# The transposes of a routed slot's rows, moved behind the transposes of h

## The reference

```
x = x + 0.5 * ffn(layernorm(x))
x = x + attn(layernorm(x))      # w_in, causal conv of 4 taps, linear recurrence of 16 states, silu, w_out
x = x + 0.5 * ffn(layernorm(x))

def ffn(x):                                  # 4096 tokens of 256, F = 512, E = 8 experts
    shared = (silu(x @ sg.T) * (x @ su.T)) @ sd.T
    e = argmax(x @ gate_w.T);  score = sigmoid(max(x @ gate_w.T))
    xs = x * score                           # each token goes to its one expert e
    routed = (silu(xs @ rg[e].T) * (xs @ ru[e].T)) @ rd[e].T
    return shared + routed
```

## Time and profile before

| | |
|---|---|
| median of 3 runs | 862.42 us (861.83 to 862.47) |
| the profiled execution's own time | 862.49 us |
| its span in the trace | 860.6 us |
| granted TensorE clock, mean | 0.99 |
| TensorE busy | 828.5 us |
| VectorE, ScalarE, GpSimd busy | 484.4, 391.5, 463.1 us |
| gate and up products (L424 to L426, with xT) | 130.2 + 122.9 + 123.4 us busy, 312 each |
| transposes of rows (L600) | 156, 0.27 us each |
| transposes of h (L631) | 312, 0.27 us each |

### The profile page before, as it was taken

How to read it: one execution, slowest core, us unless ns; L and a number is a source line. 1 busy time by engine, 2 the same in 40 slices (tenths; PEclk the granted TensorE clock), 3 DMA queues, 4 the chain that set the end, 5 groups by cost and what they waited for, 6 DMA issues and landing times.

```text
span 860.6 us, 16215 instructions
## 1 busy us (share of the span) xinstructions
PE 828.5 (96%) x5302; PEld 721.7 (84%) x5303; DVE 484.4 (56%) x981; ACT 391.5 (45%) x766; POOL 463.1 (54%) x444
## 2 busy tenths in 40 slices
PE   4999999999999999999999999999999999999995
PEld 3778988888888888888888888888888888888884
DVE  7788753333333336678999986767333333333454
ACT  4743323334334334556777786233244334343331
POOL 6528870333334058859999982687331243330684
PEclk9999999999999999998999999999999999999998
DMA  9973553646565337310010015255345555421565
GB/s 310 324 260 105 177 166 118 208 165 203 168 212 173 102 67 141 44 26 13 7 57 26 26 51 196 66 162 188 124 139 185 205 197 195 156 101 43 117 153 159
DMA packets 52389, 119.07 MB, mean 138 GB/s; under 512 B 6442, under 2 KB 40372, under 8 KB 47988
## 3 DMA queue, kind: packets, MB, share of 16 engines
q0 software_dynamic: 17008, 75.25, 27.9%
q1 hardware_dynamic: 34834, 43.15, 15.5%
q10 hardware_dynamic: 498, 0.02, 0.0%
HBM read 83.25 MB, written 35.14 MB: 138 GB/s over the span
## 4 chain that ended last, share of the span: by engine, by line
PE 72%; POOL 12%; DVE 7%; issue 3%; DMA 3%; ACT 1%; POOLq 0%; DVEq 0%; SPq 0%
PE bank L424 21%; PE bank L426 20%; PE bank L425 20%; POOL xs_sorted L1858 4%; PE bank L631 4%; DVE v L1544 3%; POOL yr L2052 3%; POOL acc L1932 2%; DMA wr_hi<-w_routed 2%; PE bank L600 2%; POOL wr_lo L1902 2%; PE bank L491 1%; PE bank L502 1%; POOL wr_lo L1894 1%; DVE stats L1226 1%
## 5 line engine op out<-in xcount | busy, mean ns | idle before, releaser
L1902 POOL TENSOR_TENSOR wr_lo<-wr_raw,wr_hi 128x3072 fp32r<-128x3072 f32 x14 | 95.4, 6818 | 96.0 <-DMA wr_hi<-w_routed 87.7
L424 PE MATMUL bank<-wr_hi,xT_hi 128*128 x312 | 130.2, 417 | 1.2 <-POOL wr_lo L1902 1.2
L1209 DVE TENSOR_TENSOR hT_lo<-bank,hT_hi 128x512 fp32r<-128x512 f32 x78 | 54.0, 692 | 124.6 <-ACT hT_hi L884 124.6
L1502 DVE TENSOR_TENSOR hf<-sg,bank 128x512 f32<-128x512 f32 x78 | 53.7, 688 | 124.3 <-PE bank L426 124.3
L426 PE MATMUL bank<-wr_lo,xT_hi 128*128 x312 | 123.4, 396 | 0.0
L425 PE MATMUL bank<-wr_hi,xT_lo 128*128 x312 | 122.9, 394 | 0.0
L1932 POOL DMA_INDIRECT acc<-ys_sorted,pos x44 | 70.8, 1609 | 79.3 <-issue 49.3
L424 PE MATMUL bank<-xT_hi,ws_hi 128*128 128x512 f32 x256 | 102.4, 400 | 2.2 <-DVE xT_lo L1209 2.2
L425 PE MATMUL bank<-xT_hi,ws_lo 128*128 128x512 f32 x256 | 100.8, 394 | 0.0
L426 PE MATMUL bank<-xT_lo,ws_hi 128*128 128x512 f32 x256 | 100.7, 393 | 0.0
L911 ACT ACTIVATE sg<-bank 128x512 f32<-128x512 f32 x64 | 38.3, 598 | 126.4 <-PE bank L426 126.3
(11 more groups left out here) (248 smaller groups left out, 2180.7 us busy)
## 6 DMA issues: line engine op xcount, KB each, us to landing
wr_raw<-w_routed POOLq DMA_DIRECT2D x16, 1536.0 KB, 7.2
wr_hi<-w_routed POOLq DMA_DIRECT2D x16, 1536.0 KB, 7.8
rows<-xs_sorted SPq DMA_DIRECT2D x78, 128.0 KB, 2.4
ys_sorted<-rows SPq DMA_DIRECT2D x78, 128.0 KB, 1.7
xg<-xT_kept SPq DMA_DIRECT2D x12, 512.0 KB, 4.2
xT_kept<-xTf SPq DMA_DIRECT2D x9, 512.0 KB, 3.2
acc<-x SPq DMA_DIRECT2D x8, 512.0 KB, 9.8
xs_sorted<-zeros POOLq DMA_DIRECT2D x4, 1024.0 KB, 8.3
```

Of the source, the lines that this page charges most:

```text
L424: pe.matmul(o, a_hi, b_hi, start=start, stop=False, skip_group_check=True)
L1209: return dve.tensor_tensor(o, full, f32(h), ALU.subtract)
L1502: dve.tensor_tensor(hf[:, 0, :], sg[:, 0, :], MU[:, :], ALU.mult).then_inc(s_mh, 1)
L1902: pool.tensor_tensor(wr_lo[:, e % 2, :], wr_raw[:, :], f32(wr_hi[:, e % 2, :]), ALU.subtract).then_inc(s_wl, 1)
```

## The change

The transposes of rows are moved. Step s becomes: down of slot s-1; transposes of h of slot s; transposes of the rows of slot s+2; gate and up of slot s+1. MXT is still read for xT_lo of slot s+1 when the transposes of slot s+2 are due, so TensorE waits for `s_mxl` first. MXT is now full long before xT_hi is free, which gate and up of the slot ahead still read, so ScalarE waits for these (`s_mu`) ahead of xT_hi. At the start of the stage, the transposes of slot 1 stand ahead of gate and up of slot 0, and the two expert numbers are loaded together.

```diff
@@ m_transpose (TensorE)
                 pe.wait_ge(s_xsl[j], 16 * (L * (NS // RING) + use + 1))
+                if not isinstance(s, int) or s > 0:
+                    pe.wait_ge(s_mxl, L * NS + s)
                 for kb in range(KB):
@@ routed_steps (TensorE)
                     s = s0 + a
-                    m_transpose(L, s + 1, (a + 2) % RING, use0 + (a + 2) // RING)
                     m_down(L, s - 1, prev)
                     if now is None:
                         now = expert_of(s)[1]
                     following = expert_of(s + 1)
                     m_transpose_h(L, s)
+                    if not isinstance(s, int) or s + 2 < NS:
+                        m_transpose(L, s + 2, (a + 3) % RING, use0 + (a + 3) // RING)
                     m_gate_up(L, s + 1, *following)
@@ routed_slots (TensorE)
-                m_gate_up(L, 0, *expert_of(0))
+                first, following = expert_of(0), expert_of(1)
                 m_transpose(L, 1, 1, 0)
-                following = expert_of(1)
+                m_gate_up(L, 0, *first)
                 m_transpose_h(L, 0)
+                m_transpose(L, 2, 2, 0)
                 m_gate_up(L, 1, *following)
@@ m_x_hi (ScalarE)
+                if not isinstance(s, int) or s > 0:
+                    act.wait_ge(s_mu, L * NS + s)
                 act.wait_ge(s_mt, L * NS + s + 1)
```

## The result

The changed kernel takes 864.71 us (median of 13 runs) beside 861.98 for the kernel before (13 runs); the ratio is 1.0028, with a 95% interval of 1.0017 to 1.0039. It is slower by some 2.4 us, where no change (862.4, range to 864.2) was forecast. The profiled execution has 864.71 us and a span of 862.9, 2.3 more than before.

The account below looks back on a forecast made before the run. TensorE, busy for 828.5 of 860.6 us, was taken as the bound. Moving the transposes cancels to 0.0, stage starts add 0.44, weight waits give back 0.44: sum 0.0, so 862.4 us, range 861.0 to 864.2.

Parts of the forecast that it names:

- part 4: Start of each stage: slot 1's transposes leave an idle hole, +0.22 us per layer, +0.44 in all; late issue priced 0.
- part 3: Waits inside a slot: hf, xT_lo and the new waits all come in time, with margins of 0.45 and 0.56 us; price nothing.
- Parts 1 and 2: Row transposes out between up and down, in behind those of h: 0.22 us each way in 74 slots, cancelling to 0.0.
- C: Rival, faster: a transpose in a longer chain costs 0.09 us, 2.2 less in all, 860.2 us; chance 0.07.
- Part 5: Two waits for expert weights: down frees the buffer sooner, each wait shrinks by 0.22 us, -0.44 in all.
- Part 6: SyncE's row loads: worst lead falls from 11.61 to 8.81 us against a slowest landing of 8.6; price 0, margin 0.2.
- B: Rival, slower: rows land late and stall their transposes; 0.3 us at all 12 weight refills gives +3.6, 866.0; chance 0.05.
- A: Rival, slower: setup behind the new wait makes gate products 0.12 us late in 74 slots, +8.9, 871.3 us; chance 0.09.
- D: Rival, slower: TensorE's clock falls with six transposes in a row; three slots at 1.2 GHz cost 14.6, 877.0; chance 0.01.

Follow-up runs that it names:

- e1: Changed kernel with TensorE's loop of nine steps written out, so no jump back: 861.95 us, ratio 0.9999 to the kernel before.
- e5: Changed kernel with the transposes of rows back ahead of down in the first step of each loop pass only: 863.06 us, ratio 1.0009.
- e9: Kernel before, order unchanged, with only the new wait for xT_lo put ahead of the transposes of rows: 862.43 us, ratio 1.0003.
- e3: Changed kernel with a loop body of three steps, 11 jumps back per layer instead of 3: 868.09 us, ratio 1.0070.
- e4: Kernel before with a loop body of three steps, 11 jumps back per layer instead of 3: 862.74 us, ratio 1.0005.
- e7: Changed kernel with the transposes of slot 1's rows back behind gate and up of slot 0: 863.98 us, ratio 1.0017.
- e8: Changed kernel with loop written out, stores one step later and slot 1's transposes back behind gate and up of slot 0: 861.57 us, ratio 0.9989.
- e11: Kernel before with TensorE's loop written out and nothing else: 860.91 us, ratio 0.9984.
- e2: Changed kernel, loop kept, with one expert-number read moved ahead of down in the first step of a pass: 864.02 us, ratio 1.0023.
- e6: Changed kernel with SyncE's stores one step later in its list, so row loads are issued sooner: 863.38 us, ratio 1.0019.

## Why the prediction was wrong

**The step that failed** is the last of part 4. The row of 134.29 with 0.18 "issue" was read as a matter of the stage's first pass: "With less work ahead of them this may grow by up to 0.22 per layer. I take 0 and keep 0.4 for the range.". In the first passes it did grow by no more than that (slot 1: 0.13 and 0.07 longer). But it is a matter of every pass, and passes two to four were priced at nothing. There TensorE's instruction stream reaches the transposes of h about 0.3 us late: 0.29 on average and 0.05 in the slot behind, six times, 2.0 us. I had compared the start of a pass with other slots (both 4.87) and taken equal for free; equal meant hidden.

What the stream does there stands in the trace too, in the rows of the instructions that TensorE's sequencer carries out itself (PEldq: a jump, a register sum, a read of slot_e). The first step of a pass has a jump (COMPARE_BRANCH, 0.2 us) and three reads of slot_e, where every other step has one read. Each read is a TENSOR_LOAD of 0.30 us, a register sum of 0.15 and a short SEQ_ASSERT, and from the start of the second read to the start of the third it takes 0.74 to 0.80 us in after. Here are the jump and the reads ahead of slot 10 of the first layer in after (count, ns min/median/max of one, first and last start in us):

```profile
L671 PEldq COMPARE_BRANCH  x1: 231/231/231, 174.0 to 174.0; - x1
...
L638 PEldq TENSOR_LOAD <-slot_e x3: 299/300/432, 174.4 to 177.3; - x3
L638 PEldq SEQ_ASSERT  x3: 18/18/18, 175.1 to 177.9; - x3
```

The last SEQ_ASSERT ends at 177.91, and the weight load of the transposes of h starts at 177.96. In all six late slots it starts 0.05 us behind this row (0.14 in the second layer, where one more register sum, for the number of the slot, stands between). So the transposes wait for the third read, which the profile calls "issue". In the kernel before the reads end 0.07 to 0.21 ahead of the weight load, which is all the cover there was. In e1 they end 0.39 to 0.53 ahead, in slot 10 of the first layer at 176.46 for a weight load at 176.99:

```profile
L638 PEldq SEQ_ASSERT  x3: 18/18/18, 174.1 to 176.4; - x3
```

The stream itself is not slower than before: from the start of the jump to the end of the third read it takes 3.77 to 3.87 us in after and 3.75 to 3.88 before. But it comes to the jump later. In the kernel before that is 0.81 us behind the first transpose of h of the slot ahead (174.10 - 173.29), in after 1.25 (174.04 - 172.79). The rows, before first:

```profile
173.29 0.60 PE L631 MATMUL bank<-ident,hf 128*128 128x128 f32 x4
...
L667 PEldq COMPARE_BRANCH  x1: 232/232/232, 174.1 to 174.1; - x1
```
```profile
172.79 0.60 PE L633 MATMUL bank<-ident,hf 128*128 128x128 f32 x4
```

These 0.44 us have two halves. One is the pair of transposes, which now stands between the transposes of h and the jump. The other belongs to part 3. In a plain slot the sequencer stands at a wait for xT_lo: its next instruction comes 0.04 to 0.05 us (median) behind the end of xT_lo, after a pause of 0.2 to 0.3. The prediction worked out rightly that xT_lo ends no sooner while the transposes of h start 0.22 sooner. So xT_lo ended 0.34 ahead of them before and 0.11 ahead of them after, and the stream goes on that much later beside the matmuls. "Price: nothing" held for the gate products, but it took from the stream's lead, which the sum has nowhere. e5, with the pair back at the start of the pass but xT_lo still 0.11 ahead, comes to the jump at 1.01 to 1.05, half way, and wins back half. e9, the old order with the new wait, has 0.34 and 0.81 as before, and no loss.

How far the cause is shown: e1 (no loop, no loss) and e3 (more jumps, more loss) tie the loss to the start of a pass, and e4 shows that the old order hides it as long as nothing else holds up the stream. That the third read is what the transposes wait for, and that the stream goes on with xT_lo, is read from the rows. No run separates the jump from the two extra reads. An estimate from the rows: one read is 0.64 us even in e1, more than the 0.29 that was lost, so carrying the two expert numbers over the jump in registers might do as well as writing the loop out; it wasn't tried.

Parts 1 and 2 (0.22 out, 0.22 in): right, 0.35 and 0.89, and plain slots at 4.87. The chain of six takes the rate of the running stream, so C didn't come.

Part 3: right for plain slots, and short of the stream's lead as said above. hf ends at 252.01, 0.44 before its use; xT_hi starts with hf at 251.32 and gains nothing; the new waits cost nothing in plain slots (also e9).

Part 4, start: the idle time grew by 0.22 per layer as worked out (0.85 against 0.63, undone by e7); no total shows the 0.44.

Part 5 (waits for weights shorter by 0.44): not confirmed. In the changed kernel they fell by 1.17, more than the order gives. The slots between release and use had become longer by the losses above, which would do that, at least in part. In e8, where these losses are gone, they sum to 1.78 over 4.87 (0.62, 0.31, 0.85) against 1.66 before and 1.39 in e11. From the issue of wr_hi to the start of wr_lo, the three chains of concern scatter between 7.1 and 8.4 us over these runs, which is wider than the 0.22 looked for.

Part 6: the lead of 8.81 was right (8.80). The price was wrong, since the 8.6 of one execution is not the worst case: 9.1, 9.2 and 8.7 came in this one, and the slowest of the other kernels' executions is between 7.5 (e9) and 9.7 (e2). Three slots paid 1.36. This is B, with fewer loads and a larger price each than I gave it. The longer lead of e6 mends it.

A didn't come where I put it, ahead of the gate products, but its kind did: an instruction stream that is late where older work no longer covers it. The total would have been worse still, had the waits for weights not given back 1.17 where 0.44 was forecast. D: the granted clock stayed at 1.00 with six transposes in a row (1.00 from 135 to 315 and from 620 to 795 us). The Trainium skill, "TensorE: Matmul & The Clock Gate", Part 4 (PE-mode transpose), would have had the full-clock state not engaged by such work; no run here shows a loss of that kind.

## What to carry to other kernels

The work at the head of a loop body may be covering the restart of its instruction stream. Before moving it, read the rows of the sequencer: when the last instruction that it carries out itself ends, and when the work behind it starts. That distance (0.07 to 0.21 us here) is the margin, and equal lengths of the steps don't show it. Or write the loop out and see. And where an operand is asked for earlier, weigh the new lead against the slowest landing of several executions, with a margin; one execution's maximum is none.

## What the runs showed that was not expected

Writing TensorE's loop out (e11) made the old kernel faster, 0.9984 (0.9975 to 0.9993), though the trace of before shows no loss at the starts of passes two to four. Of the 1.8 us of span, 0.6 lie in the first stage (186.31 against 186.91), and none in the second. Most of the first is its two shorter waits for weights (1.22 over 4.87 against 1.66), which scatter by as much between executions, and slot 1, the first pass (5.11 against 5.24). In the second stage slot 1 gains 0.12 too, and slot 18 loses 0.17. The other 1.2 us lie outside the routed stages and were not traced to a place. The price is more instructions to fetch. Queue q8 of before, then of e11 (kind: packets, MB, share of 16 engines):

```profile
q8 instruction: 31, 0.51, 0.2%
```
```profile
q8 instruction: 48, 0.79, 0.4%
```
